# Ternarising feed-forward weights inside the last head group, and tile normalisations on ScalarE

## The chip, the core and the metric

The kernel runs on one core of a Trainium2 chip. The time is device microseconds of one execution. Engines: PE is TensorE, DVE is VectorE, ACT is ScalarE, POOL is GpSimd, SP is the engine that here only issues DMAs.

## The reference

One decoder layer, post-norm, on x of 4 batches x 512 rows x 512 columns, with a layernorm after each residual sum:

1. attention over the feature axis (stage A below);
2. fused self and cross attention with 16 query heads in 8 groups, fp8-rounded inputs and weights, layernorm on each head's q and k (stage B);
3. a feed-forward block whose weights are ternary and whose rows are rounded to integers (stage C):

```python
def _quant_weight(w):
    scale = jnp.clip(jnp.mean(jnp.abs(w)), EPS, None)
    return jnp.clip(jnp.round(w / scale), -1.0, 1.0) * scale
def _quant_act(x):
    scale = 127.0 / jnp.clip(jnp.max(jnp.abs(x), axis=-1, keepdims=True), EPS, None)
    return jnp.clip(jnp.round(x * scale), -128.0, 127.0) / scale
h = bitlinear(x, w_gate_up)            # 512 -> 4096
a, b = jnp.split(h, 2, axis=-1)
h = jax.nn.silu(a) * b
out = _layernorm(x + bitlinear(h, w_down))   # 2048 -> 512
```

(The straight-through terms of the reference are left out here, and `bitlinear` is a product of the rounded rows and rounded weights.) The scale of a weight matrix is a mean over all of it, so no weight can be ternarised before every absolute value has been summed.

## The kernel before

All engines run lists of instructions written out by hand, in order, with semaphores between them; what stands first in an engine's list is done first, even if it has to wait.

**Stage A** takes the first 440 us or so and ends with XQ: the normalised rows, transposed and fp8-rounded in four versions (for q, cross q, k and v). XQ takes 64 KB of each partition.

**Stage B** is a loop over 32 pairs n = 4g + b: head group g (8 of them) and batch b (4). Each pair has four steps st (128 rows each), counted through as T = 4n + st, 0 to 127. In one step PE makes the scores of two heads, the projections of the next pair n + 1 (they read XQ and the weights split in high and low f16 halves: `whq`/`wlq` in two slots, g mod 2), the products of probabilities and values of step T - 1, transposes of probabilities, and the output projection of step T - 2. DVE accumulates the output projection of T - 3 (or T - 2) into x1 (L1086), takes row maxima (L1111), normalises q and k (L1056), scales probabilities (L1066), and rounds the attention rows to fp8 in five operations (L1072 to L1082). ACT makes the exponentials (L805) and copies from PSUM. POOL computes reciprocal deviations. In the last group nothing has to be prepared for a next one; in the last pair there are no projections. x1 is complete for batch b once pair 28 + b has been accumulated.

In each pair ACT also sums absolute values of a 1/32 slice of the feed-forward weights (L785, L786; loads `load_abs` on SP).

**Between B and C.** After the last step DVE adds up these sums, POOL reduces over partitions, and DVE makes the scale (L1162 to L1165). The weights, 12 chunks of 128 x 2048 f32 (1 MB each), are loaded to `wch`, which has 8 slots and lies over stage B's buffers, after the last projection. A chunk is ternarised in three operations: scale and add 1.5 x 2^23 on DVE (`tern_scale`, L1239), subtract it again into bf16 on ACT (L888), clip to -1 and 1 on DVE (`tern_clip`, L1243). 8 chunks are the gate and up weights `wgu`, 4 the down weights `wdn`.

**Stage C** has 16 tiles t of 128 rows. For each: statistics of x1's rows (`x_stats`, L1174, L1177), POOL's deviation (L1356, L1358), normalisation (L1193), row maximum, scales, rounding (`x_prepare`, L1193 to L1201), ACT's subtraction (L865), transposes (L617). Then 32 matmuls of gate and up in four quarters j (L632); ACT's silu of each quarter (L871) and DVE's product (`h_make`, L1207); the maximum over the whole hidden row (L1212), scales, four roundings (L1219), ACT's subtractions (L877), 16 transposes (L642), two copies to hT (ACT), 16 down matmuls (L651), then y (L1225), its statistics, POOL's deviation, normalisation (`y_out`, L1234) and the store. The order is written out in `two_tiles`: PE does the whole of gate and up of tile t + 1, then all transposes of tile t, then its down product. DVE does the reduction and the four roundings of tile t, y of tile t - 1, then the products of tile t + 1 with `x_prepare(t + 2)` behind the second.

## Time and profile before

| | us |
|---|---|
| median of 3 runs (1930.96 to 1931.54) | 1931.26 |
| the profiled execution, its own time | 1932.42 |
| its span, first to last instruction | 1930.6 |

Over the span PE is busy 1790.4 us (93%), DVE 1525.8 (79%), ACT 1052.5 (55%), POOL 262.9 (14%). How to read it: busy time is the sum over instructions, with overlaps taken once; a group's mean duration is longer than the distance from one start to the next when instructions follow each other closely, so the costs of a queue are read from start to start. In a row of a stretch the numbers after its length are busy us and, in brackets, instructions of PE, PE's weight loads, DVE, ACT and POOL, in this order. The clock column behind them is the TensorE clock that was granted, 1.00 being 2.4 GHz and 0.50 being 1.2 GHz.

### The profile page before, as it was taken

How to read it: one execution, taken by the hardware profiler on the slowest of the kernel's cores; microseconds unless marked ns; L12 is line 12 of the kernel's file. 1: busy time of each engine (PE TensorE's matmuls, PEld its weight loads, DVE VectorE, ACT ScalarE, POOL GpSimd, SP SyncE). 2: the span in 40 equal slices, each digit the busy share in tenths (PEclk: the TensorE clock that was granted, in tenths of full speed). 3: DMA queues.
4: the chain of work that ended last, by engine and by line, in shares of the span. 5: the costliest groups of instructions: out<-in, count | busy, mean ns of one | idle time of the engine just before them, and what ended most of it. 6: DMA issues, size and time to landing. Idle time of an engine off the chain costs nothing.

```text
span 1930.6 us, 32318 instructions
## 1 busy us (share of the span) xinstructions
PE 1790.4 (93%) x11024; PEld 1245.1 (64%) x11024; DVE 1525.8 (79%) x4964; ACT 1052.5 (55%) x2526; POOL 262.9 (14%) x361
## 2 busy tenths in 40 slices
PE   7999999448999999999999999999999999759987
PEld 3444444236877777877877877787787887424443
DVE  0175747487888888888898888888889888789997
ACT  1121211225667666776666666766677566566555
POOL 0000000011111112111111111211111111111110
PEclk9999999769999999999999999999999999979999
DMA  6000000201101110100101110111010000420000
GB/s 218 22 1 22 1 0 1 78 1 61 44 22 39 33 33 10 54 28 22 54 20 30 39 36 22 39 33 33 21 51 9 11 11 24 175 81 17 23 23 28
DMA packets 46209, 70.79 MB, mean 37 GB/s; under 512 B 3552, under 2 KB 26592, under 8 KB 45024
## 3 DMA queue, kind: packets, MB, share of 16 engines
q1 hardware_dynamic: 46048, 68.73, 10.7%
q8 instruction: 90, 1.47, 0.3%
q14 instruction: 71, 0.58, 0.1%
HBM read 63.47 MB, written 4.19 MB: 35 GB/s over the span
## 4 chain that ended last, share of the span: by engine, by line
PE 75%; DVE 16%; ACT 5%; issue 2%; DMA 1%; POOL 1%; DVEq 0%; POOLq 0%; ACTq 0%; SPq 0%
PE bank L354 17%; PE bank L410 16%; PE bank L464 10%; PE bank L512 9%; PE bank L549 5%; PE bank L476 5%; PE bank L585 3%; PE bank L470 3%; PE bank L443 3%; DVE am L1212 2%; PE bank L437 1%; ACT hb L877 1%; PE bank L632 1%; DVE hh L1207 1%; ACT hs L871 1%
## 5 line engine op out<-in xcount | busy, mean ns | idle before, releaser
L805 ACT ACTIVATE pr<-bank,nmx 128x512 f32<-128x512 f32 x256 | 175.2, 693 | 148.3 <-DVE nmx L1111 148.2
L512 PE MATMUL bank<-kT,qT 128*128 128x512 f32 x512 | 242.4, 596 | 0.7 <-ACT kT L756 0.7
L464 PE MATMUL bank<-prT,KV 128*128 128x256 f32 x1024 | 242.3, 379 | 0.5 <-ACT prT L680 0.4
L410 PE MATMUL bank<-whq,XQ 128*128 128x256 f16 x1024 | 234.7, 276 | 0.0
L410 PE MATMUL bank<-wlq,XQ 128*128 128x256 f16 x1024 | 234.5, 275 | 0.0
L464 PEld LDWEIGHTS bank<-prT,KV 128*128 128x128 f32 x1024 | 189.5, 190 | 52.5 <-issue 23.0
L1324 POOL TENSOR_TENSOR rdev<-gvar,cst 128x7 f32<-128x7 f32 x128 | 190.2, 1486 | 10.0
L793 ACT ACTIVATE yb<-bank,rsT 128x128 bf16<-128x128 f32 x512 | 146.7, 373 | 66.8 <-PE bank L470 66.8
L1111 DVE TENSOR_REDUCE nmx<-bank 128x1 f32<-128x512 f32 x256 | 167.1, 681 | 8.7 <-PE bank L512 5.2
L1322 POOL TENSOR_TENSOR gvar<-mvB,geps 128x7 f32<-128x7 f32 x128 | 27.3, 214 | 1046.0 <-DVE mvB L1046 1046.0
L680 ACT ACTIVATE prT<-bank 128x512 f32<-128x512 f32 x256 | 153.1, 617 | 13.3 <-PE bank L549 13.3
L549 PE MATMUL bank<-identf,pr 128*128 128x128 f32 x1024 | 150.5, 275 | 9.2 <-DVE pr L1066 8.6
L680 ACT ACTIVATE raw<-bank 128x512 f32<-128x512 f32 x128 | 76.8, 600 | 125.7 <-DVE nq L1056 66.5
L1056 DVE TENSOR_SCALAR nq<-raw,mvB,rdev 128x128 f32<-128x128 f32 x512 | 142.1, 342 | 0.7 <-POOL rdev L1324 0.7
L512 PEld LDWEIGHTS bank<-kT,qT 128*128 128x128 f32 x512 | 92.7, 191 | 72.2 <-issue 61.8
L410 PE MATMUL bank<-whk,XQ 128*128 128x128 f16 x1024 | 126.7, 221 | 9.8 <-DVE wlk L1025 8.6
L476 PE MATMUL bank<-wp,cq 128*128 128x512 bf16 x512 | 132.3, 381 | 2.9 <-DVE x L1086 2.9
L549 PEld LDWEIGHTS bank<-identf,pr 128*128 128x128 f32 x1024 | 118.8, 142 | 23.7 <-DVE pr L1066 21.3
L750 ACT ACTIVATE qT<-bank,hlq 128x256 f32<-128x256 f32 x256 | 133.3, 588 | 1.2 <-PE bank L443 1.1
L1066 DVE TENSOR_SCALAR pr<-pr,ri 128x512 f32<-128x512 f32 x256 | 124.5, 487 | 9.1
L632 PE MATMUL bank<-wgu,xiT 128*128 128x512 bf16 x512 | 119.9, 390 | 9.9 <-ACT hs L871 6.5
L410 PE MATMUL bank<-wlk,XQ 128*128 128x128 f16 x1024 | 126.7, 221 | 0.0
(163 smaller groups left out, 3447.5 us busy)
## 6 DMA issues: line engine op xcount, KB each, us to landing
wst<-in_wcat SPq DMA_DIRECT2D x24, 512.0 KB, 4.0
wpst<-in_wproj SPq DMA_DIRECT2D x8, 1024.0 KB, 5.3
wa<-in_wgu SPq DMA_DIRECT2D x32, 256.0 KB, 2.6
wch<-in_wgu SPq DMA_DIRECT2D x8, 1024.0 KB, 13.2
xT<-in_xT SPq DMA_DIRECT2D x4, 1024.0 KB, 5.3
x<-in_x SPq DMA_DIRECT2D x4, 1024.0 KB, 12.1
wkx<-in_wkvx SPq DMA_DIRECT2D x8, 512.0 KB, 5.0
wa<-in_wdn SPq DMA_DIRECT2D x32, 128.0 KB, 2.6
```

The source lines that it names most:

```text
L354: ins = mm(dst, lhs(k), rhs(k), start=(k == 0), stop=(k == n - 1))
L410: ins = mm(dst, XQ[:, c, k, b * S + j * P:b * S + (j + 1) * P], w, start=(k == 0 and m == 0), stop=(k == KT - 1 and m == 1))
L464: mm(OB[:, 0:2 * P], KV[:, n % 2, t, P:2 * P], prT[:, st % 2, t, :, :].rearrange("p h s -> p (h s)"), start=(t == 0), stop=(t == ST - 1))
L476: ins = mm(P0[:, :], cq[:, T % 2, c * P:(c + 1) * P], wp[:, c, :], start=(c == 0), stop=(c == 3))
L512: mm(SB_[h][:], qT[:, h, st * P:(st + 1) * P], kT[:, :], start=True, stop=True).then_inc(s["scores_made"], 1)
L549: ins = nc.tensor.transpose(TB_[h][:, t * P:(t + 1) * P], pr[:, h, t * P:(t + 1) * P], identf[:])
L680: return act_f(dst, src, ACT.Copy)
L793: ins = act_f(yb[:, T % 2, c * P:(c + 1) * P], OB[:, c * P:(c + 1) * P], ACT.Copy, scale=rsT[:, T // 16, c:c + 1])
L805: act_f(pr[:, h, :], SB_[h][:], ACT.Exp, bias=nmx[:, st, h:h + 1], accum_out=su[:, st, h:h + 1]).then_inc(s["exp_done"], 1)
L1056: ins = v.tensor_scalar(nq[:, j % 2, h * P:(h + 1) * P], raw[:, h * P:(h + 1) * P], mvB[:, h, 0:1], rdev[:, h:h + 1], ALU.subtract, ALU.mult)
L1111: v.tensor_reduce(nmx[:, st, h:h + 1], SB_[h][:], AX.X, ALU.max, negate=True).then_inc(s["max_ready"], 1)
L1324: g.tensor_tensor(rdev[:], gvar[:], CPOW, ALU.pow).then_inc(s["stats_ready"], 1)
```

## The change

1. **Memory.** XQ is laid out by batch. In the last group a batch's part is free once its pair is projected, and `wgu` and `wdn` are written over it. `wch` is gone: chunks are staged in two places that are free in the last group, `wst` (even chunks) and slot 0 of the split weights, now one tensor `wqs` (odd ones).
2. **Sums of absolutes** come in 24 loads of 128 x 1024 in pairs 0 to 23, in place of 32 of 128 x 512 and 128 x 256; POOL's reduction over partitions stands in pair 24, the scale on DVE in pair 25.
3. **Ternarising** is spread by a table TURN over steps of pairs 28 to 31: two chunks in pair 28, three each in 29 and 30, four in 31. In such a step DVE clips the chunk before and scales this one, after rounding the attention rows; ACT subtracts after its probability copies. SP loads chunk c + 2 when ACT has done chunk c.
4. **First tiles.** In the last pair DVE also does `x_stats(0..3)` and, in steps 1 to 3, `x_prepare(0..2)`; ACT the normalisations of tiles 0 to 2 and the subtractions of 0 and 1; PE transposes tile 0 in the last step. PE starts gate and up of tile 0 between the last two output projections.
5. **Normalisations on ACT.** x and y are normalised by an Identity activation with scale 1/deviation and bias -mean/deviation; POOL makes that bias in two more operations.
6. **Order of the loop.** PE puts the first half of tile t's transposes between the third and fourth gate quarter of t + 1, and the second half behind the fourth. DVE puts the four roundings behind the first product, y behind the second and `x_prepare(t + 3)` behind the third. The statistics run four tiles ahead. y has two buffers, xiT three, the scales four.

The diff, cut to its core:

```diff
+NCH = 12
+TURN = {(28, 2): 0, (28, 3): 1, (29, 1): 2, (29, 2): 3, (29, 3): 4, (30, 1): 5, (30, 2): 6, (30, 3): 7,
+        (31, 0): 8, (31, 1): 9, (31, 2): 10, (31, 3): 11}
-        XQ = sb(stageAB, "XQ", [P, 4, KT, NB * S], BF16)
+        XQ = sb(stageAB, "XQ", [P, NB, 4, KT, S], BF16)
-        wch = sb(stC, "wch", [P, NCH, F])
+        def stage(c):
+            if c % 2 == 0:
+                return wst[:, :, :, :].rearrange("p s k n -> p (s k n)")
+            return wqs[:, 0, :, :, :].rearrange("p a k n -> p (a k n)").bitcast(F32)
...
# SP
+            def load_chunk(c):
+                if c < 2:
+                    sp.wait_ge(s["wl_ready"], 6 * NG)
+                    sp.wait_ge(s["proj_q_made"], 4 * (TT - 4))
+                else:
+                    sp.wait_ge(s["tern_int"], c - 1)
...
+                sp.dma_start(dst, src).then_inc(chunk_loaded[c % 2], 16)
...
+                if n == TT - 5:
+                    load_chunk(0)
+                    load_chunk(1)
+                for st in range(ST):
+                    if (n, st) in TURN and TURN[n, st] + 2 < NCH:
+                        load_chunk(TURN[n, st] + 2)
...
# PE, stage C
+            av(LT - 1)
+            pe.wait_ge(s["acc_done"], LT - 2)
+            project_out(LT - 2)
+            turn_x(1, 1)
+            pe.wait_ge(s["tern_made"], 8)
+            gate_up(0, 0, 0, True)
+            gate_up(0, 0, 1, True)
+            pe.wait_ge(s["acc_done"], LT - 1)
+            project_out(LT - 1)
+            gate_up(0, 0, 2, True)
+            gate_up(0, 0, 3, True)
...
+            for t in range(NT):
+                for j in range(4):
+                    if t + 1 < NT:
+                        gate_up(t + 1, (t + 1) % 2, j, False)
+                    if j in (2, 3):
+                        turn_h(t, j - 2)
+                if t + 2 < NT:
+                    turn_x(t + 2, t % 2)
+                down(t)
...
# ACT, pair of stage B
+                    if n == TT - 1 and st == 2:
+                        xi_out(0, 0)
+                    if n == TT - 1 and st == 3:
+                        xt_out(0, 0)
+                        xi_out(1, 1)
+                    if n == TT - 1 and st:
+                        x_norm(st - 1)
+                    if (n, st) in TURN:
+                        tern_out(TURN[n, st])
...
# ACT, stage C
+            for t in range(NT):
+                for j in range(4):
+                    if t + 1 < NT:
+                        silu(t + 1, (t + 1) % 2, j)
+                    if j == 1:
+                        for i in range(4):
+                            hb_out(t, i, t == 0)
+                        if t + 3 < NT:
+                            x_norm(t + 3)
+                    if j in (2, 3):
+                        h_out(t, j - 2)
+                if t + 2 < NT:
+                    xt_out(t + 2, t % 2)
+                if t + 3 < NT:
+                    xi_out(t + 3, (t + 1) % 2)
+                if t:
+                    y_norm(t - 1, (t - 1) % 2)
+            y_norm(NT - 1, 1)
...
+            def x_norm(t):
+                act.wait_ge(s["rstdX_ready"], t + 1)
+                act_f(x1[:, t, :], x1[:, t, :], ACT.Identity, scale=rsC[:, 0:1], bias=nbC[:, 0:1]).then_inc(s["xn_done"], 1)
...
# DVE, pair of stage B
+                    if (n, st) in TURN:
+                        c = TURN[n, st]
+                        if c:
+                            tern_clip(c - 1)
+                        tern_scale(c)
+                    if n == TT - 1 and st:
+                        x_prepare(st - 1, (st - 1) % 2)
+                    if n == TT - 1:
+                        x_stats(st)
...
# DVE, x_prepare: its own normalisation is gone
-                dve.wait_ge(s["rstdX_ready"], t + 1)
-                own.do(v.tensor_scalar(x1[:, t, :], x1[:, t, :], mvC[:, 0, 0:1], rsC[:, 0:1], ALU.subtract, ALU.mult))
+                dve.wait_ge(s["xn_done"], t + 1)
...
# DVE, stage C
+            h_make(0, 0, 0)
+            h_make(0, 0, 1)
+            accumulate(LT - 1, 15)
+            h_make(0, 0, 2)
+            h_make(0, 0, 3)
+            for t in range(NT):
+                h_scales(t, t % 2)
+                for j in range(4):
+                    if t + 1 < NT:
+                        h_make(t + 1, (t + 1) % 2, j)
+                    if j == 0:
+                        for i in range(4):
+                            h_round(t, t % 2, i, t == 0)
+                    if j == 1 and t:
+                        y_make(t - 1, (t - 1) % 2)
+                    if j == 2 and t + 3 < NT:
+                        x_prepare(t + 3, (t + 1) % 2)
+                if t + 4 < NT:
+                    x_stats(t + 4)
+            y_make(NT - 1, 1)
```

## Rows read from the trace of the kernel before

**Rows 1.** The page, chain that ended last, shares by engine.
```profile
PE 75%; DVE 16%; ACT 5%; issue 2%; DMA 1%; POOL 1%; DVEq 0%; POOLq 0%; ACTq 0%; SPq 0%
```

**Rows 2.** Stretches of the run: window, busy per engine (instructions), granted clock, DMA share, GB/s.
```profile
1538.20:1653.80 115.60, 114.09 (x824) 90.57 (x822) 99.36 (x355) 75.74 (x195) 20.46 (x24) 1.00 0.16 61
1644.50:1674.50 30.00, 26.27 (x138) 18.74 (x137) 22.88 (x59) 17.52 (x49) 0.20 (x1) 1.00 0.54 224
1674.50:1719.35 44.85, 15.38 (x63) 6.61 (x62) 35.21 (x65) 29.01 (x25) 8.76 (x7) 0.66 0.27 94
1719.35:1903.12 183.77, 163.99 (x934) 78.43 (x932) 164.17 (x371) 104.95 (x167) 19.29 (x52) 0.98 0.05 18
```

**Rows 3.** Groups of instructions in 1674.5 to 1719.35: count, busy us, mean ns, idle before.
```profile
L1239 DVE TENSOR_SCALAR wch<-wch,winv 128x2048 f32<-128x2048 f32 x12 | 15.2, 1276 | 0.0
L888 ACT ACTIVATE wgu<-wch 128x2048 bf16<-128x2048 f32 x8 | 15.0, 1900 | 11.7 <-DVE wch L1239 11.7
L1243 DVE TENSOR_SCALAR wgu<-wgu 128x2048 bf16<-128x2048 bf16 x8 | 5.5, 690 | 0.0
```

**Rows 4.** Timeline of DVE, pair 29: start, duration, instruction, idle before.
```profile
1597.15 0.75 DVE L1086 SCALAR_TENSOR_TENSOR x<-bank,pscale,x 128x512 f32<-128x512 f32 x1
...
1603.96 0.29 DVE L1072 TENSOR_SCALAR yb<-yb 128x512 bf16<-128x512 bf16 x1 [0.74 <-ACT yb L793]
...
1608.94 0.48 DVE L1066 TENSOR_SCALAR pr<-pr,ri 128x512 f32<-128x512 f32 x1
...
1614.18 0.69 DVE L1132 TENSOR_REDUCE xmx<-bank 128x8 f32<-128x512 f32 x1 [1.19 <-PE bank L585]
```

**Rows 5.** Timeline of PE, the same pair.
```profile
1596.95 1.88 PE L512 MATMUL bank<-kT,qT 128*128 128x512 f32 x4
...
1609.95 0.60 PE L549 MATMUL bank<-identf,pr 128*128 128x128 f32 x4
```

**Rows 6.** Timeline of DVE, one tile of the feed-forward loop.
```profile
1799.05 2.25 DVE L1212 TENSOR_REDUCE am<-hh 128x1 f32<-128x2048 f32 x1
...
1803.43 0.75 DVE L1225 SCALAR_TENSOR_TENSOR y<-bank,am,x 128x512 f32<-128x512 f32 x1
...
1805.22 1.41 DVE L1207 SCALAR_TENSOR_TENSOR hh<-bank,am,hs 128x512 f32<-128x512 f32 x2
1806.55 0.54 DVE L1193 TENSOR_SCALAR x<-x,mvC,rsC 128x512 f32<-128x512 f32 x1
1807.13 0.68 DVE L1196 TENSOR_REDUCE am<-x 128x1 f32<-128x512 f32 x1
...
1808.75 0.74 DVE L1207 SCALAR_TENSOR_TENSOR hh<-bank,am,hs 128x512 f32<-128x512 f32 x1
...
1811.19 0.54 DVE L1234 TENSOR_SCALAR yo<-y,mvC,rsC 128x512 f32<-128x512 f32 x1
...
1812.47 2.25 DVE L1212 TENSOR_REDUCE am<-hh 128x1 f32<-128x2048 f32 x1
```

**Rows 7.** Timeline of PE behind the last pair.
```profile
1679.87 1.89 PE L476 MATMUL bank<-wp,cq 128*128 128x512 bf16 x4 [2.94 <-DVE x L1086]
...
1706.95 5.42 PE L632 MATMUL bank<-wgu,xiT 128*128 128x512 bf16 x16 [2.92 <-DVE wgu L1243]
```

**Rows 8.** Waits in 1759 to 1890: who for whom, us in total, times, longest.
```profile
PE bank L651 <- ACT hT L680: 13.0, 11, 1.2
```

**Rows 9.** Line 1212, the reduction over a hidden tile: duration ns, first and last start.
```profile
L1212 DVE TENSOR_REDUCE am<-hh x16: 2253/2253/2286, 1719.3 to 1914.6; 128x1 f32<-128x2048 f32 x16
```

**Rows 10.** Timeline of POOL, one tile.
```profile
1812.63 0.19 POOL L1356 TENSOR_TENSOR vC<-mvC,cst 128x1 f32<-128x1 f32 x1 [6.61 <-DVE mvC L1177]
```

**Rows 11.** Groups of the whole run, line 756.
```profile
L756 ACT ACTIVATE kT<-bank,hln 128x512 f32<-128x512 f32 x32 | 25.5, 796 | 1.2 <-PE bank L449 1.2
```

**Rows 12.** Groups of the whole run, table loads.
```profile
L680 ACT ACT_TABLE_LOAD x1 | 1.3, 1283 | 15.6 <-PE bank L354 15.6
L871 ACT ACT_TABLE_LOAD x1 | 1.3, 1283 | 0.0
```

More of the change, by code:

```diff
@@ L471, in av, with turn_x @@
                 ins.then_inc(s["av_made"], 1)
+            def turn_x(t, par):
+                pe.wait_ge(s["xi_made"], t + 1)
+                if par or not (isinstance(t, int) and t == 0):
+                    pe.wait_ge(s["xit_out"], t)
+                for k in range(KT):
+                    ins = nc.tensor.transpose(MBh[:, k * P:(k + 1) * P], xib[:, k * P:(k + 1) * P], identb[:])
+                ins.then_inc(s["xit_made"], 1)
             def project_out(T):
@@ L647, in down, with turn_h @@
+            def turn_h(t, u):
+                pe.wait_ge(s["hb_ready"], 4 * t + 2 * u + 2)
+                if t:
+                    pe.wait_ge(s["ht_out"], 2 * t + (u - 1))
+                half = bank[4 + u][:, :].bitcast(BF16)
+                for c in range(8):
+                    ins = nc.tensor.transpose(half[:, c * P:(c + 1) * P], hb[:, (8 * u + c) * P:(8 * u + c + 1) * P], identb[:])
+                ins.then_inc(s["ht_made"], 1)
+            def down(t):
+                if t:
                     pe.wait_ge(s["y_ready"], t)
@@ L877, in hb_out @@
                 act_f(hb[:, j * D:(j + 1) * D], hi_[:, j * D:(j + 1) * D], ACT.Copy, bias=-INT_ROUND).then_inc(s["hb_ready"], 1)
-            def h_out(t, first):
-                for u in range(2):
-                    act.wait_ge(s["ht_made"], 2 * t + u + 1)
-                    if u == 0 and not first:
-                        act.wait_ge(s["dn_made"], t)
-                    copy(hT[:, 8 * u:8 * u + 8, :], bank[4 + u][:, :].bitcast(BF16).rearrange("p (c s) -> p c s", c=8)).then_inc(s["ht_out"], 1)
@@ L893, in _, with y_norm @@
+            def y_norm(t, par):
+                act.wait_ge(s["rstdY_ready"], t + 1)
+                if t >= 2:
+                    act.wait_ge(out_stored[par], 16 * (t // 2))
+                act_f(yo[:, par], y[:, par], ACT.Identity, scale=rsC[:, 1:2], bias=nbC[:, 1:2]).then_inc(s["yo_ready"], 1)
+            xt_out(1, 1)
+            xi_out(2, 0)
             for j in range(4):
                 silu(0, 0, j, True)
-            def two_tiles(t0, first, last):
-                for par in range(2):
-                    t = t0 + par
-                    f = first and par == 0
-                    more = not (last and par == 1)
-                    for j in range(4):
-                        hb_out(t, j, f)
-                    for j in range(4):
-                        if more:
-                            silu(t + 1, 1 - par, j)
-                        if j == 2 and not last:
-                            xi_out(t + 2, par)
-                    h_out(t, f)
-                    if not last:
-                        xt_out(t + 2, par)
@@ new lines, in x_stats, with x_prepare @@
+            def x_stats(t):
+                stats(x1[:, t, :], 0, s["varX_ready"])
+            def x_prepare(t, par):
+                dve.wait_ge(s["xn_done"], t + 1)
+                own.do(v.tensor_reduce(am[:, 0, 0:1], x1[:, t, :], AX.X, ALU.max, apply_absolute_value=True))
+                own.sync()
+                scales(t, 0)
+                if par or not (isinstance(t, int) and t == 0):
+                    dve.wait_ge(s["xi_made"], t)
+                v.tensor_scalar(xi[:], x1[:, t, :], am2[:, t % 4, 2:3], INT_ROUND, ALU.mult, ALU.add).then_inc(s["xi_added"], 1)
@@ L1213, in h_scales @@
                 own.sync()
-                scales(par, 1)
+                scales(t, 1)
             def h_round(t, par, j, first):
```

360 lines of the change are left out of this document (136 added, 224 removed).

## The prediction

> **What bounds the kernel now.** I read the page's chain first: three quarters of it is TensorE, 16% VectorE [rows 1]. An average over stages is no use for a change at the end, so next came the table of stretches [rows 2]. Three regimes are to be seen. In head pairs 28 to 30 (1538.2 to 1653.8) PE is busy 114.1 of 115.6 us and DVE 99.4: PE-bound, DVE with little room. In the last pair, without projections, PE has 26.3 of 30.0 and DVE 22.9. From 1674.5 to the first reduction over a hidden tile at 1719.35 PE has 15.4 of 44.9 at a granted clock of 0.66: this stretch belongs to ternarising and the first tiles. In the tile loop PE and DVE are level, 164.0 and 164.2 of 183.8 us, 11.7 each per tile, yet a tile takes 13.1.
>
> **What the ternarising costs.** A chunk is one scaling (1.28 us), one ScalarE copy (1.90) and one clip (0.69) [rows 3]; on DVE scaling and clip take 1.8 start to start. Twelve are 21.6 us of DVE and 22.8 of ACT. The change removes none of it, but moves it under pairs 28 to 31, with the preparation of tiles 0 to 2 and the statistics of tiles 0 to 3.
>
> **Pairs 28 to 30: plus 9.9 us.** In DVE's order the chunk stands ahead of the next accumulation and the next row maxima, and PE waits for both. The margins: accumulation L1086 ends at 1597.9, and PE reaches the projection that needs it after its scores L512 (1596.95 and 1.88, less an overlap), at about 1598.7: 0.8 us. The scaled rows L1066 end at 1609.4, PE's transposes L549 start at 1609.95: 0.5. DVE's idle gaps behind those places are 0.74 before L1072 and 1.19 before L1132 [rows 4, 5]. Pair 29, three chunks: after the first, DVE is 1.8 late and PE hardly; after the second 3.6, the accumulation arrives 2.8 beyond its margin and PE is 2.8 late; the 0.74 gap closes; after the third DVE is 4.65 late and PE 4.15. So 5.4 us of work gives 4.1 of delay. Pair 30 likewise 4.1; pair 28, with one scaling (its clip comes later) and one whole chunk (3.0 us), 1.7. ACT's copy starts when the scaling ends and takes 1.9, while DVE comes to the next maximum after 1.4; the exponentials are so 0.5 later than DVE's own delay, and DVE needs them only after its normalisations, so I price that at nothing. Bounds: 4 us, if the margins hold at every step, and 26, where each chunk costs DVE and ACT in series (8 x 3.7 less three times 1.2). I take 9.9, nearest to the margins read.
>
> **Last pair: plus 14.0 us.** Step 0 gets a chunk and one tile's statistics (1.8 + 0.82), of which the 1.19 gap takes up one part: 1.4. Steps 1 to 3 get chunk, preparation (1.62 without its normalisation) and statistics: 4.3 each [rows 6]; of the waits there only about 0.5 is given back, so 12.6. Bounds: 10 (twice as much given back) to 20 (PE, idle for some 4 us per step, falls to 1.2 GHz and its part of the chain doubles). ACT's normalisation (0.8) fits before the preparation, since DVE first does 1.8 of chunk.
>
> **Tail: 13.6 us in place of 44.85.** From the end of pair 31 on DVE, now 1674.5 + 23.9 = 1698.4: accumulation 0.7; PE has by then been idle for over 10 us and starts at 1.2 GHz, as in the trace, where the last output projection took 1.89 and the first 16 gate matmuls 5.42, both behind a long gap [rows 7]. So: projection 1.9, transposes 0.6, eight matmuls 3.4, eight more 1.9 with the clock returning, projection 0.9, sixteen 3.4, last product 0.8. ACT's table load falls beside the first matmuls. First hidden reduction at 1712.0 instead of 1719.35. **Net of these three: minus 7.3.**
>
> **Tile loop and end: minus 21.1 us.** One tile of DVE, from each start to the next [rows 6]: reduction, scales and four roundings 4.38; y and its statistics 1.79; two products 1.33; x normalisation 0.58; rest of the preparation 1.62; y normalisation and x statistics 1.28, of which 0.46 is the first (0.54 less the overlap) and 0.82 the second. With two further products and a wait for ACT's silu this is 13.1 to 13.4. The change takes out 0.58 and 0.46, and the wait, since rounding stands between the products: DVE needs 4.38 + 1.79 + 4 x 0.68 + 1.62 + 0.82 = 11.3. PE needs its 11.7 [rows 2]; what it waited was 13.0 us in ten tiles for hT before the down projection [rows 8], and this goes as well: the first eight transposes now stand before the last gate quarter, whose 1.7 us covers the copy of the first half, and eight down matmuls cover the second. ACT is busy 105.0 us in the 14 tiles [rows 2], 7.5 each, and 8.9 with two normalisations of 0.7 net. Between DVE's 11.3 and PE's 11.7 I take PE's, plus 0.7 once for the first tile: 14 x 11.7 + 0.7 = 164.5 where it was 183.8. The last interval has no preparation: 9.1 for 11.5, since the reductions run from 1719.3 to 1914.6 [rows 9]. The end behind it was 16.0; two more short POOL operations (0.19 each, [rows 10], with their signals about 0.5) and the slower engine make it 16.6. So 190.2 for 211.3.
>
> Is it right to give ScalarE the normalisation? The row speaks against it operation by operation: DVE takes 0.54 [rows 6], ACT's Identity with two per-row operands 0.80 [rows 11]. By price alone the change would lose 0.26 x 32 = 8 us; as DVE is 13.1 long and ACT 8.9, I count it as a gain of 1.0 per tile. The Trainium skill ("ScalarE: Activation LUTs", Rules for kernel authors) says to use VectorE, not ScalarE, for multiply and add. By that rule the loop would not get shorter by this edit; the trace agrees with its price, and not with its use here.
>
> Elsewhere: sums of absolutes go from 32 loads to 24 of the same total size, free before and after (ACT is busy 75.7 of 115.6 us in the pairs), the new layout of XQ changes no instruction's size, and SP's queue reaches each chunk load two steps before it is needed. At nothing; if a load came late, DVE would stand in front of everything in the last pair.
>
> **Sum.** -7.3 - 21.1 = -28.4. The profiled execution took 1932.4 (span 1930.6), 1.2 above the median of 1931.3. From the median: 1903.
>
> **Rivals.**
> *Pairs stall in series.* Each chunk delays PE by DVE's 1.8 and ACT's 1.9. For it: DVE is busy 86% there and its idle gaps are waits of a chain; against: DVE doesn't need the exponentials at once. 16 us more: 1919. Chance 0.17.
> *The tile stays bound by a chain.* Reduction, rounding, ACT's copies, then x normalisation ahead of the third silu, in one ACT queue: if the third silu comes 0.9 late in each tile, 12.6 per tile: +12.6, 1915. For: ACT starts rounding only when DVE gives it; against: by my times the silu and DVE arrive together. Chance 0.15.
> *Slower: tables.* ACT loaded a table twice in the whole run, at the start and before the first silu, 1.28 each [rows 12]. Identity ran with Exp's table; no row shows it with Silu's. If they do not share one, each tile has Silu to Identity and back twice: 4 x 1.28 = 5.1 on ACT, 14.0 per tile, over 13.1 from the second load on and so slower than before: 14 x 14.0 = 196, and with the loads in the tail and end about 1938. The change would then not move the normalisation off the path but lengthen it. The Trainium skill (same page, Table sets: the hidden batching unit) says cheap functions such as identity are in every set; by it this rival falls. Chance 0.03.
> *Both first rivals at once*: 1931, no change. 0.03.
> *Better*: DVE's work in the pairs hides (4 instead of 9.9) or the loop goes below PE's count: 1893 to 1898. 0.10.
> The forecast itself keeps 0.52.
>
> **How the numbers follow.** Range: low 1893 (pairs at 4 and last pair at 10). High 1918: nearly reaches the first rival and holds the second. About 0.2 is outside. A measurement of this kernel can tell some 0.2%, 4 us: faster 0.94 (the forecast, the first two rivals and the better case), same 0.03 (both rivals), slower 0.03 (tables).
>
> **What would show it.** Right: the ternarising copies lie between about 1540 and 1690, three per pair, and pairs 29 and 30 are 42 to 43 us long; the first hidden reduction starts at 1712 +- 5; the reductions are 11.7 apart; DVE no longer waits for silu and PE's wait for hT is gone; still two table loads. Wrong: pairs of over 46 us, a DVE wait for ACT's x normalisation or for a chunk load in the last pair, intervals over 12.3 in the loop, or more than two table loads.

## The result, and the profile after

The changed kernel takes 1904.17 us (median of 4 runs, 1903.54 to 1905.79) where the kernel before, beside it, takes 1931.4 (1930.96 to 1931.68): a ratio of 0.986, 95% interval 0.984 to 0.988. Forecast were 1903, and a range of 1893 to 1918. The profiled execution took 1905.79, with a span of 1902.8 (before: 1932.42 and 1930.6), so the difference to be found in the two traces is 27.8 us of span.

To cut both traces at the same places I use two instructions that occur once in each unit of work: the exponential of the cross scores (px, once per pair, in its first step) and the reduction over a hidden tile (once per tile).

| from start to start | before | after | difference | forecast |
|---|---|---|---|---|
| start to px of pair 24 | 1382.44 | 1381.40 | -1.0 | 0 |
| px 24 to px 25 | 39.12 | 45.47 | +6.35 | 0 |
| px 25 to px 28 | 116.69 | 116.68 | 0.0 | 0 |
| px 28 to px 31 | 115.52 | 128.53 | +13.0 | +11.3 |
| px 31 to first hidden reduction | 65.58 | 44.50 | -21.1 | -18.65 |
| first to last hidden reduction | 195.28 | 169.60 | -25.7 | -21.7 |
| last hidden reduction to the end | 16.0 | 16.6 | +0.6 | +0.6 |
| sum | | | -27.8 | -28.4 |

The forecast of each row regroups its terms (step 0 of the last pair, 1.4, belongs to the row of px 28 to px 31). The start to px 24 is where single executions differ: 1380.1 to 1382.9 over the kernels of this study. The sum is right within 1 us, its parts are not: +6.35 in pair 24 was priced at nothing, and the last pair with the tail and the tile loop gave 2.45 and 4.0 more than forecast. The 4.0 hides two errors of its own: the 14 tiles up to the last reduction but one took 158.1 us where 164.5 were forecast, and the last interval took 11.48 where 9.1 were forecast.

The table of stretches of the kernel after (columns as in [rows 2]); the stretches are px 24 to px 25, px 28 to px 31, px 31 to the first reduction, and 14 tiles:

```profile
1381.40:1426.87 45.47, 41.40 (x282) 32.94 (x280) 34.65 (x123) 27.56 (x70) 7.33 (x9) 0.92 0.10 30
1543.55:1672.08 128.53, 117.65 (x824) 90.96 (x821) 114.37 (x374) 87.48 (x191) 26.14 (x28) 0.99 0.20 67
1672.08:1716.58 44.50, 33.53 (x149) 21.99 (x150) 34.90 (x82) 27.46 (x52) 3.21 (x12) 0.88 0.13 48
1716.58:1874.70 158.12, 157.24 (x936) 79.41 (x934) 147.05 (x321) 120.51 (x191) 26.66 (x100) 1.00 0.06 21
```

The last line answers to the last of [rows 2]: 14 tiles take 158.1 in place of 183.8 us, and PE is busy in all but 0.9 of them. DVE has gone from 164.2 to 147.1, ACT from 105.0 to 120.5. The second line shows the price: in the pairs PE now stands 10.9 us of 128.5, where it stood 1.5 of 115.6. The third: the 33.5 us of PE work between px 31 and the first hidden reduction (33.1 before) now lie in 44.5 us and no longer in 65.6.

**The tile loop.** The waits of 58 us of it (1795 to 1853), which answer to [rows 8]:

```profile
POOL vC L1364 <- DVE mvC L1136: 45.2, 10, 6.1
ACT hs L901 <- PE bank L640: 13.2, 10, 1.6
DVE hh L1257 <- ACT hs L901: 1.7, 5, 0.3
```

PE waits for nobody there; its wait for hT (13.0 us before) is gone. DVE's timeline over one tile, against [rows 6]:

```profile
1796.55 2.25 DVE L1262 TENSOR_REDUCE am<-hh 128x1 f32<-128x2048 f32 x1
...
1800.01 1.67 DVE L1269 TENSOR_SCALAR hi_<-hh,am 128x512 f32<-128x512 f32 x4
...
1804.27 0.75 DVE L1257 SCALAR_TENSOR_TENSOR hh<-bank,am,hs 128x512 f32<-128x512 f32 x1 [0.33 <-ACT hs L901]
...
1808.03 2.25 DVE L1262 TENSOR_REDUCE am<-hh 128x1 f32<-128x2048 f32 x1
```

11.48 from reduction to reduction, with one gap of 0.33 us in front of a product. DVE would need 11.15, PE's work fills 11.48: the bound is PE. The same work looked like more in the kernel before. Four of its inner tiles:

```profile
1825.54:1877.80 52.26, 47.35 (x274) 22.70 (x272) 47.63 (x109) 30.19 (x49) 5.93 (x16) 1.00 0.06 21
```

PE is busy 11.84 per tile there, at a granted clock of 1.00 as in after; the 0.98 of [rows 2] comes from the first tile alone, 0.76 from 1719.35 to 1733.40. A gate or down matmul follows the one before it by 216 ns in both kernels. Nearly all of the 0.36 between 11.84 and 11.48 is in the records of two matmuls: in these tiles of before PE stops twice (1.18 us for hT, 0.05 between two gate quarters), and the record of the matmul in front of each stop is 0.16 longer than where the next one follows at once.

**The tail.** It begins with DVE's first accumulation behind the last pair, forecast 33.3 us after px 31 and found 33.9 after it:

```profile
1705.95 0.72 DVE L1114 SCALAR_TENSOR_TENSOR x<-bank,pscale,x 128x512 f32<-128x512 f32 x1
```

Where [rows 7] show the first 16 gate matmuls in 5.42 us, PE's timeline of after has

```profile
1706.72 1.04 PE L498 MATMUL bank<-wp,cq 128*128 128x512 bf16 x4 [1.94 <-DVE x L1114]
1707.60 0.39 PE L492 MATMUL bank<-identb,xib 128*128 128x128 bf16 x4
1707.82 3.62 PE L640 MATMUL bank<-wgu,xiT 128*128 128x512 bf16 x16
```

The projection takes 1.04 (1.89 before) and the gate 3.62: both as long as at the upper level of the clock. PE had waited 1.9 us before them, where in the kernel before it had worked 5.6 us of the 32.5 from 1674.5 to 1707.

**Pair 24.** POOL's timeline around the reduction over partitions, and the waits beside it:

```profile
1391.77 1.53 POOL L1335 TENSOR_TENSOR rdev<-gvar,cst 128x7 f32<-128x7 f32 x1
1399.17 0.41 POOL L1346 PARTITION_ALL_REDUCE asum<-asum  x1 [5.87 <-issue]
1406.94 0.20 POOL L1333 TENSOR_TENSOR gvar<-mvB,geps 128x7 f32<-128x7 f32 x1 [7.37 <-issue]
```

```profile
POOL gvar L1333 <- issue: 7.4, 1, 7.4
...
DVE kn L1082 <- POOL rdev L1335: 5.4, 1, 5.4
...
PE bank L463 <- DVE nq L1084: 3.7, 1, 3.7
```

An operation of 0.41 us occupies POOL for 13.6 us, since it stands still for 5.9 in front of it and 7.4 behind, though the next deviation's input is there 5.8 us before it starts. That deviation of q and k comes late, DVE waits 5.4 us for it, PE 3.7 for DVE, and the granted clock of the pair is 0.92 where before it was 1.00 throughout. PE stands 4.07 us in this pair (0.43 before) and is busy 41.40 (38.69 before): of the 6.35, some 3.6 are waiting and 2.7 the lower clock. The five kernels of this study that have the reduction in step 1 took 43.7 to 45.7 for this pair, so 6.35 is near the upper end of what it costs (4.6 to 6.6).

**Pairs 28 to 30.** Pair 28 (two chunks) is 1.66 longer, pair 29 (three) 4.08, as forecast (1.7 and 4.1). The third interval, pair 30 and step 0 of pair 31, is 7.27 longer, forecast 5.5. PE's timeline in pair 30 shows what was added:

```profile
1642.20 1.91 PE L424 MATMUL bank<-wqs,XQ 128*128 128x256 f16 x16
...
1650.61 2.83 PE L424 MATMUL bank<-wqs,XQ 128*128 128x256 f16 x16 [2.16 <-DVE x L1114]
1653.24 2.69 PE L478 MATMUL bank<-prT,KV 128*128 128x256 f32 x8
```

Behind a wait of 2.16 us for DVE's accumulation the same sixteen projections take 2.83 in place of 1.91, and eight products of probabilities and values 2.69 in place of 1.89 (both at full clock one step before): 1.7 us by the lower clock. A wait of this size does not always have that effect. In pair 29 PE waits 2.05 us at the same place, both in after and in the kernel of experiment 3 below, whose instructions up to there are the same. The pair in after, and in that kernel:

```profile
1584.06:1626.68 42.62, 39.20 (x292) 31.01 (x291) 38.38 (x126) 28.50 (x62) 8.55 (x8) 1.00 0.23 75
```

```profile
1581.49:1625.77 44.28, 40.70 (x289) 32.04 (x290) 38.47 (x126) 28.51 (x62) 8.55 (x8) 0.96 0.21 73
```

The second one's clock fell and its pair is 1.66 longer. A difference of up to 1.7 us between single stretches of two traces can be this alone.

ACT loaded a table twice, as in [rows 12], and Identity in the loop costs what the row of before said (0.80):

```profile
L816 ACT ACTIVATE x<-x,nbC,rsC 128x512 f32<-128x512 f32 x16 | 12.9, 804 | 0.0
L692 ACT ACT_TABLE_LOAD x1 | 1.3, 1283 | 14.7 <-PE bank L368 14.7
L901 ACT ACT_TABLE_LOAD x1 | 1.3, 1283 | 0.0
```

### The profile page after: what moved, and what is told of

The parts are those of the page before. It is cut to its first block, busy times and chain, and to the rows that moved or that the text cites. A ratio compares the mean times of both kernels' runs of the same rounds, so it can differ in the third digit from the quotient of the medians.

```text
span 1902.8 us, 32280 instructions
## 1 busy us (share of the span) xinstructions
PE 1789.1 (94%) x11024; PEld 1251.0 (66%) x11024; DVE 1506.1 (79%) x4917; ACT 1065.9 (56%) x2478; POOL 269.1 (14%) x417
## 3 DMA queue, kind: packets, MB, share of 16 engines
q1 hardware_dynamic: 40288, 68.73, 10.9%
## 4 chain that ended last, share of the span: by engine, by line
PE 71%; DVE 15%; issue 8%; POOL 2%; ACT 2%; DMA 1%; POOLq 0%; SPq 0%; DVEq 0%; ACTq 0%
PE bank L368 18%; PE bank L424 14%; PE bank L478 10%; PE bank L534 8%; PE bank L573 5%; PE bank L498 4%; PE bank L609 3%; PE bank L484 3%; PE bank L457 2%; PE bank L451 1%; DVE nq L1084 1%; DVE nmx L1190 1%; ACT yb L823 1%; PE bank L542 1%; POOL rsC L1369 1%
## 5 line engine op out<-in xcount | busy, mean ns | idle before, releaser
L424 PE MATMUL bank<-wqs,XQ 128*128 128x256 f16 x2048 | 249.5, 276 | 4.4 <-DVE x L1114 4.4
L424 PEld LDWEIGHTS bank<-wqs,XQ 128*128 128x128 bf16 x2048 | 199.6, 100 | 45.4 <-issue 15.7
L640 PE MATMUL bank<-wgu,xiT 128*128 128x512 bf16 x512 | 115.7, 379 | 0.1
```

The lines of the kernel that those rows point to most:

```text
L424: ins = mm(dst, XQ[:, b, c, k, j * P:(j + 1) * P], w, start=(k == 0 and m == 0), stop=(k == KT - 1 and m == 1))
```

## The experiments

Each kernel is the one after the change with the edit shown. The span of the profiled execution stands in brackets behind the time.

**1. POOL's reduction where POOL has room.** Behind the fourth deviation of a pair POOL is idle for some 15 us (its longest wait for DVE in 1543 to 1672 is 16.4).

```diff
-                    if n == NABS and st == 1:
+                    if n == NABS and st == 3:
                         pool.wait_ge(s["abs_ready"], 1)
```

> The changed kernel with one edit: POOL's reduction over partitions stands behind the deviation of step 3 of pair 24, not of step 1. Theory: in the changed kernel this reduction kept POOL for 13.6 us (5.9 of issue before it, 7.4 behind it), the next deviation came 5.7 late and pair 24 took 45.5 us in place of 39.1. Behind step 3 POOL has 16.6 us until its next work, so the pair goes back to 39.1 and the kernel gets 6.3 us faster, about 1898. Rival: pair 24 is long for another reason (DVE's two sums, the load of the absolutes' last slice); then it stays at 45 and the time at 1904. Second rival: the 13.6 us run over into step 0 of pair 25 and the wait moves there: pair 24 at 39, pair 25 longer by up to 6.

1898.38 us (1897.74 to 1899.97; span 1896.9), ratio to before 0.983, interval 0.982 to 0.984. px 24 to px 25 is 39.13 again, every later interval is within 0.02 us what it was in after. POOL's timeline:

```profile
1407.90 1.48 POOL L1335 TENSOR_TENSOR rdev<-gvar,cst 128x7 f32<-128x7 f32 x1
1415.38 0.41 POOL L1346 PARTITION_ALL_REDUCE asum<-asum  x1 [6.01 <-issue]
1425.06 0.21 POOL L1333 TENSOR_TENSOR gvar<-mvB,geps 128x7 f32<-128x7 f32 x1 [9.27 <-DVE mvB L1074]
```

The 6.0 in front are there again, but the next deviation now waits for its data (it starts 0.09 us after them), and no longer for POOL. So the lengthening of pair 24 is the place of this one instruction. Its second rival falls too, since px 25 to px 28 is 116.69 as before. With it in step 3 the change brings 33.5 us (beside 1931.89) in place of 27.2.

**2. What belongs to the reduction and what to the change of kind**, on top of experiment 1.

```diff
+                        own.do(g.partition_all_reduce(asum3[:], asum2[:], P, RADD))
+                        own.sync()
                         g.partition_all_reduce(asum3[:], asum2[:], P, RADD).then_inc(s["absum_ready"], 1)
```

> e1_reduce_gap (1898.4 us) with POOL's reduction over partitions issued twice in a row, the second from the same source to the same place. My theory: the 5.9 us before the reduction and the 7.4 behind it belong to the change of POOL from ordinary operations to this one and back, not to the operation, so the second one starts within a microsecond of the end of the first, and the whole stays at 1898 to 1899. Rival: each reduction carries its own 5.9 in front; then the second starts 6 us after the first, POOL comes back to its deviations about 1429.6 where e1_reduce_gap began the next at 1425.1, DVE and PE wait, and the whole is 4 to 5 us longer, 1903.

1899.31 us in one run (span 1897.2). POOL's timeline:

```profile
1415.96 0.43 POOL L1346 PARTITION_ALL_REDUCE asum<-asum  x1 [5.98 <-issue]
1416.50 0.40 POOL L1348 PARTITION_ALL_REDUCE asum<-asum  x1
1425.67 0.21 POOL L1333 TENSOR_TENSOR gvar<-mvB,geps 128x7 f32<-128x7 f32 x1 [8.77 <-DVE mvB L1074]
```

The second starts 0.54 us after the start of the first, and it had to wait until the first was complete. The 6 us belong to the first use after other operations, not to each reduction; and the stillness behind is not the reduction itself running on longer than its record of 0.41 says. What the stillness behind is made of no run shows: here the next deviation waits for its data, 8.8 us. The Trainium skill ("GPSIMD Engine Reference", Instruction dispatch) says that the first call to a freshly loaded kernel pays about 6 us for the loading of its code, with no instruction to be seen in the profile; the trace agrees, with 5.9 to 6.0 in three kernels. But it was not this program's first reduction: one stands in stage A, at 16.9 us in after, and the price was paid anew. In the kernel before, POOL's timeline has the reduction between the stages:

```profile
1668.39 0.20 POOL L1335 TENSOR_TENSOR asum<-asum 128x8 f32<-128x8 f32 x1 [25.18 <-ACT wa L786]
1674.71 0.41 POOL L1351 PARTITION_ALL_REDUCE asum<-asum  x1 [6.12 <-DVE asum L1157]
1683.66 1.13 POOL L1356 TENSOR_TENSOR vC<-mvC,cst 128x1 f32<-128x1 f32 x1 [8.54 <-DVE mvC L1177]
```

It had been idle for 6.1 us when the sums came, and the reduction started 0.14 us after them; and it was idle for 8.5 behind it until the next statistics, and started 0.09 after those: whatever both sides cost lay under waits.

**3. Normalisations of the loop back on DVE**, all else as in after.

```diff
# ACT, stage C
-                        if t + 3 < NT:
-                            x_norm(t + 3)
-                if t:
-                    y_norm(t - 1, (t - 1) % 2)
-            y_norm(NT - 1, 1)
# DVE, x_prepare from t = 3 on; y likewise ahead of x_stats(t + 4)
+                    v.tensor_scalar(x1[:, t, :], x1[:, t, :], mvC[:, 0, 0:1], rsC[:, 0:1], ALU.subtract, ALU.mult).then_inc(s["xn_done"], 1)
```

> The changed kernel with the normalisations of the tile loop (x of tiles 3 to 15, y of all) back on VectorE, each 0.54 us; everything else, the new order too, as changed. Theory: PE's 11.5 per tile is the bound after the change and DVE is at 11.3; with 1.04 more DVE is at 12.35 and becomes the bound, so tiles come every 12.4 us and the kernel is 10 to 13 us slower than the changed one, about 1916. Rival: the order of the loop alone brought the gain and DVE's queue still has room: 11.5 to 11.7 per tile and 1904 to 1907.

1910.53 us (1910.33 to 1911.85; span 1908.7), ratio 0.989, interval 0.988 to 0.991. The tiles are 12.08 apart. Ten of them, in the table of stretches:

```profile
1738.68:1859.32 120.64, 115.77 (x668) 57.24 (x681) 116.93 (x259) 76.57 (x120) 22.27 (x80) 1.00 0.06 23
```

DVE is busy 116.9 and PE 115.8 of 120.6, and PE waits for the rounded rows again. First to last reduction is 176.0 in place of 169.6: 6.4 us for the whole loop, which is also the difference of the medians. (In the two traces pair 24 is 1.75 shorter and pair 29, by its clock, 1.66 longer; the two nearly cancel, and the end is 0.7 longer.) So of the 1.6 us per tile that the change takes out, the new order alone gives 1.0 (13.07 to 12.08) and the normalisations 0.6 (to 11.48). I had put the latter at 1.0, and this experiment at 10 to 13 us.

**4. PE's transposes of the hidden tile all behind the fourth gate quarter**, and ACT's copies behind the fourth silu.

```diff
-                    if j in (2, 3):
-                        turn_h(t, j - 2)
+                turn_h(t, 0)
+                turn_h(t, 1)
```

> The changed kernel with PE's old place for the transposes of the hidden tile (all 16 behind the fourth gate quarter) and ACT's two copies to hT behind its fourth silu. Theory: PE again waits about 1.2 us per tile for hT before the down product, so 12.5 to 12.7 per tile and 15 us slower, about 1919. Rival: what made PE wait was DVE's length, and with the normalisations gone from DVE the place of the transposes does not matter: 11.5 to 11.8 per tile, 1904 to 1908.

1913.93 us in one run (span 1911.8), tiles 12.17 apart. The waits in the loop of this kernel:

```profile
PE bank L658 <- ACT hT L692: 3.8, 5, 0.8
DVE hh L1257 <- PE bank L640: 3.6, 5, 0.7
```

PE's wait for hT before the down product is back, 0.76 per tile, and with it the 0.69 by which a tile is longer. That splitting the transposes is what removes it, is so shown by itself. The tile is 0.4 shorter than I expected, since the wait is 0.76 per tile here and 13.0 / 11 = 1.2 in [rows 8].

**5. Is it DVE or ACT that makes the pairs longer?** The scalings and clips in pairs 28 to 30 are cut to 8 of 2048 columns, with ACT's copies at full size; so most of the gate and up weights stay unternarised.

```diff
-                            tern_clip(c - 1)
-                        tern_scale(c)
+                            tern_clip(c - 1, n < TT - 1)
+                        tern_scale(c, n < TT - 1)
```

> The changed kernel with DVE's scalings and clips of the chunks in pairs 28 to 30 cut to 8 of 2048 columns (so most gate and up weights are not ternarised); ACT's copies and the loads stay whole. Theory: the delay there (from the exponential of pair 28 to that of pair 31 it takes 128.5 us, 115.5 before the change) comes from DVE's 1.8 us per chunk standing ahead of the accumulation and the maxima; ACT's 1.9 are hidden. Then the stretch is 117 us or less (step 0 of pair 31 still carries its chunk), 11 us gained, about 1893. Rival (each chunk costs DVE and ACT in series): ACT's 8 x 1.9 stay on the path and the stretch is 122 to 125.

1893.13 us in one run (span 1891.3). The stretch px 28 to px 31:

```profile
1543.48:1660.54 117.06, 113.82 (x815) 90.51 (x821) 103.03 (x374) 87.18 (x192) 21.61 (x28) 1.00 0.22 74
```

117.1 in place of 128.5. Pairs 28 and 29 take 38.86 and 38.52, what they took before (38.86 and 38.52), with ACT's copies of 1.9 us in them. ACT's part was free, DVE's was all of it: 11.5 us for 8 chunks (with what the waits bring by the clock). The third interval is 39.67 where it was 38.13; the 1.5 over are the full chunk and the statistics in step 0 of pair 31, forecast 1.4.

**6. Accumulation ahead of the chunk.** If DVE's delay reaches PE by certain places only, moving the nearest one should help.

```diff
                     if (n, st) in TURN:
                         c = TURN[n, st]
+                        if st:
+                            accumulate(T - 2, (T - 2) % 16)
```

(and the same accumulation is left out at the start of the next step)

> Edit: in the steps with a chunk (but for the first step of a pair) DVE accumulates the output projection of T - 2 ahead of the clip and the scaling, in place of at the start of the next step. Nothing else is changed, POOL's reduction stays in step 1 of pair 24. My theory: the two places at which a chunk makes PE late are the accumulation (PE's next output projection waits for it) and the row maxima; with the first one ahead of the chunk, only the second is left, which had 0.5 us of room where the accumulation had 0.8. PE's wait of 2.2 us for the accumulation in pair 30 goes, and with it the granted clock of 0.66 right behind it. Pairs 28 to 30 and step 0 of pair 31 come to about 124 us in place of 128.5, the whole to 1900 to 1901. Rival A: DVE's 1.8 us per chunk reach PE by the maxima in any case, and the place of the accumulation changes nothing: 128 and 1904. Rival B: the output projection of T - 2 is not ready when DVE gets there, so that DVE waits in front of the chunk: over 130 and 1906 or more, with a DVE wait for PE's bank at the accumulation in the rows.

1907.1 us in one run (span 1905.2): nothing gained. px 28 to px 31 is 129.05. The end behind the last hidden reduction is 1.7 longer than in after, though nothing was edited there: the last 16 down matmuls take 5.30 in place of 3.61, behind the same waits, at the lower clock. The waits in 1540 to 1672 of this kernel,

```profile
PEld bank L573 <- DVE pr L1094: 9.5, 9, 2.4
PE bank L573 <- DVE pr L1094: 6.2, 5, 1.9
PEld bank L424 <- DVE x L1114: 2.7, 2, 1.6
```

and those of 1543 to 1672 in after:

```profile
PEld bank L424 <- DVE x L1114: 6.9, 3, 3.0
PEld bank L573 <- DVE pr L1094: 5.7, 5, 1.5
PE bank L424 <- DVE x L1114: 4.4, 3, 2.2
PE bank L573 <- DVE pr L1094: 3.7, 5, 1.0
```

PE's wait for the accumulation has shrunk and its wait for the scaled probabilities has grown by nearly as much. PE's wait in pair 30 is 0.73 in place of 2.16, and the lower clock behind it is gone, as six us of both traces show (first after, then this kernel; the clock stands third from the end):

```profile
1650.00:1656.00 6.00, 5.39 (x27) 4.36 (x28) 5.31 (x21) 3.77 (x6) 1.65 (x3) 0.72 0.48 161
```

```profile
1650.00:1656.00 6.00, 4.87 (x34) 4.07 (x34) 5.77 (x15) 3.47 (x6) 2.31 (x2) 1.00 0.07 9
1650.76 1.92 PE L424 MATMUL bank<-wqs,XQ 128*128 128x256 f16 x16 [0.73 <-DVE x L1114]
```

This third interval is 0.8 shorter; pairs 28 and 29 are 0.4 and 0.9 longer, with the clock at 1.00 in both kernels. Rival A holds: the place is not what matters. That DVE's sum is what does fits this and experiment 5. With experiment 1 together:

> The edit of e6_acc_first together with the one of e1_reduce_gap (POOL's reduction in step 3 of pair 24). The two act in stretches that are 150 us apart and share no wait, so their gains should add: 1898.4 less what e6_acc_first gains. By my theory 1894 to 1895, by rival A 1898, by rival B over 1900.

1898.92 us (1897.84 to 1902.26; span 1896.9), ratio 0.984, interval 0.982 to 0.985: the same as experiment 1, as rival A has it. The three intervals are as with experiment 6 alone (40.95, 43.52, 44.63), and so is the long end.

**7. Three chunks out of the last pair**, on top of experiment 1.

```diff
-TURN = {(28, 2): 0, (28, 3): 1, (29, 1): 2, (29, 2): 3, (29, 3): 4, (30, 1): 5, (30, 2): 6, (30, 3): 7,
-        (31, 0): 8, (31, 1): 9, (31, 2): 10, (31, 3): 11}
+TURN = {(28, 1): 0, (28, 2): 1, (28, 3): 2, (29, 0): 3, (29, 1): 4, (29, 2): 5, (29, 3): 6, (30, 0): 7,
+        (30, 1): 8, (30, 2): 9, (30, 3): 10, (31, 0): 11}
```

> e1_reduce_gap (1898.4 us) with another table of chunks: (28,1) to (28,3) have 0 to 2, (29,0) to (29,3) 3 to 6, (30,0) to (30,3) 7 to 10, and (31,0) has 11. Three chunks leave steps 1 to 3 of the last pair and go to pairs 28, 29 and 30. My theory: a chunk in the last pair costs all of DVE's 1.8 us, since DVE is the bound there, and one in the pairs with projections 4.08 / 3 = 1.36, the measured lengthening of pair 29 by its three: 3 x (1.36 - 1.8) = -1.3, and 1897. Rival A: the first step of a pair has 1.2 us of idle DVE before the maxima of the cross scores, so chunks there cost only about 0.6: -3.6 in all, 1895. Rival B: in the first step the clip and scaling stand ahead of the cross softmax and ACT's copy ahead of its exponential, so that a chunk there costs both engines' 1.8 and 1.9 in series: +5, 1903. Last pair to first hidden reduction: 44.5 less 5.4 by all three, so about 39 to 40.

1902.67 us (1901.67 to 1904.22; span 1899.8), ratio 0.985, interval 0.984 to 0.986: 4.3 slower than experiment 1, near rival B. The last pair with the tail gave back 3.4 (41.15 for 44.52), not 5.4: 1.1 per chunk. px 28 to px 31 went from 128.55 to 135.17, so three more chunks cost 6.6 there, 2.2 each, more than DVE's own 1.8. They do not cost the same: a chunk in step 0 stands ahead of px, so the first interval has two more (43.48 for 40.53, 1.5 each), the second one more (46.28 for 42.62, 3.7) and the third as many as before (45.41 for 45.40). One thing speaks for rival B's series, ACT's timeline in step 0 of pair 29:

```profile
1578.25 1.91 ACT L802 ACTIVATE wgu<-wqs 128x2048 bf16<-128x2048 f32 x1 [1.84 <-DVE wqs L1162]
...
1580.79 0.63 ACT L881 ACTIVATE px<-px 128x512 f32<-128x512 f32 x1
```

ACT waits 1.84 for DVE's scaling, then copies, and only then comes to the exponential of the cross scores. Another thing can explain the amount as well: the second interval's granted clock is 0.97 where it was 1.00, and in pair 29 of experiment 3 such a fall was worth 1.66 with no chunk added. Without that much, the three cost some 1.65 each. The two were not separated by a run. In the first interval, where two more chunks cost 3.0 together, rival B's 3.7 for the one in step 0 is not borne out, though its time came near. Nor did a chunk in the last pair cost 1.8, as my theory had it.

**8. The scaling on ACT**, on top of experiment 1. If DVE's sum is the price, the scaling should leave DVE.

```diff
# ACT, tern_out
+                act_f(stage(c), stage(c), ACT.Identity, scale=winv[:, w:w + 1], bias=cst[:, 6, 0:1]).then_inc(s["tern_scaled"], 1)
# DVE
-                        tern_scale(c)
```

> e1_reduce_gap (1898.4 us) with the scaling of all twelve chunks taken from DVE and put on ACT, as an Identity activation with scale 1/mean and bias 1.5 x 2^23, directly ahead of ACT's subtraction; DVE keeps the clip. My theory, from e4_no_dve_part and e6_acc_first: what makes the pairs long is the sum of DVE's work, wherever it stands, and ACT has room. In after's rows of 1543 to 1672 ACT waits 13.1 us in all in front of the 8 subtractions for DVE's scaling (1.6 each), so that with 1.9 of its own in place of the wait it ends 0.3 later per chunk. DVE loses 1.2 of 1.8 per chunk, and the 0.6 left is about its margin: pairs 28 to 30 with step 0 of pair 31 come to 118 to 120 us in place of 128.5, the last pair and the tail to about 42 in place of 44.5, and the whole to 1886 to 1889. Rival: ACT is the next bound of a step, since in 9 of 12 steps it does not wait for the maxima before its exponentials; each chunk then costs its 1.9 us more of ACT, three of them 5.7 in a pair against the 4.1 of DVE: 129 to 133, and 1898 to 1903.

1894.16 us (1893.33 to 1895.66; span 1891.5), ratio 0.981, interval 0.980 to 0.982. The best of the kernels that compute everything, by 4.2 us against experiment 1. The two intervals overlap by 0.001, but the slowest of its four runs (1895.66) is faster than the fastest of experiment 1 (1897.74). The traces say where the gain is: 2.5 in the pairs (126.04 for 128.55), 1.4 in the last pair and the tail (43.15 for 44.52). Most of the 2.5 goes with the clock. Pair 28 is even longer (41.39 for 40.53), pair 29 is 0.5 shorter, and the third interval takes 42.58 in place of 45.40 at a granted clock of 1.00 in place of 0.96: PE's wait for the accumulation in pair 30 is 1.34 there, and the fall of the clock (1.7 by the rows above) does not come. I had forecast 1886 to 1889. From the groups of ACT (6 of the 12 scalings), and the waits of 1537 to 1660:

```profile
L804 ACT ACTIVATE wqs<-wqs,cst,winv 128x2048 f32<-128x2048 f32 x6 | 12.9, 2142 | 0.0
```

```profile
DVE ri L1096 <- ACT pr L839: 8.4, 8, 1.8
PEld bank L573 <- DVE pr L1098: 7.0, 4, 2.3
```

The scaling takes ACT 2.14 us, not 1.9, and a wait that after did not have among its long ones is now there: DVE waits eight times, 8.4 us in all, for ACT's exponential. ACT was free while its part was one copy (experiment 5) and is a second bound with two operations per chunk.

> The same for chunks 0 to 7 alone; chunks 8 to 11, in the last pair, are scaled by DVE as in the kernel after. It tells the two places apart. My theory: the pairs as in e10_act_scale (118 to 120 us), the last pair and the tail as in e1_reduce_gap (44.5): 1888 to 1891, 2 us over e10_act_scale. Rival: in the last pair ACT also has the normalisations of tiles 0 to 2 and the rounding of tiles 0 and 1, which DVE's preparation waits for; 1.9 us more ahead of the next step's exponentials there cost more than DVE's 1.2 gave, and this kernel is 1 to 3 us faster than e10_act_scale.

1897.33 us (1896.38 to 1899.27; span 1897.2), ratio 0.982, interval 0.981 to 0.984. Pairs 28 and 29 as in the kernel with all twelve (41.41 and 42.10), then 43.40 up to px 31 and 45.40 from there to the first hidden reduction, against 42.58 and 43.15. So in the last pair, too, it is better to have the scaling on ACT, by about 3 us (3.2 by the medians, and no runs of the two overlap); the rival of this run falls. Against experiment 1 the first eight alone bring about 1 us, and there the runs do overlap: most of the gain comes from the last four.

## Why the prediction was right

Its sum of -28.4 against -27.8 measured is partly luck: +6.35 not priced and +1.7 too little in the pairs stand against 4.0 and 2.45 too little gain behind them, and 1.0 of the start. The forecast of the time, 1903 for 1904.17, is so close because these cancel. By its steps:

- **Pairs 28 to 30, plus 9.9.** The mechanism and the method hold. With margins of 0.8 and 0.5 and gaps of 0.74 and 1.19 read from [rows 4, 5], two chunks cost 1.66 and three 4.08 (forecast 1.7 and 4.1). What is nothing in it, ACT's copy, is nothing (experiment 5), which settles the rival of a stall in series for this table of chunks. Pair 30 was forecast 4.1 and came to 5.7: the third interval of 45.40 against 39.67 in experiment 5. The 1.6 agrees with the lower clock behind PE's wait of 2.16 (1.7 by its rows). The step had taken PE's waiting as time lost once, and not as something that also slows what comes behind it.
- **Last pair and tail, 14.0 and 13.6.** DVE's first accumulation behind the last pair starts 33.9 after px 31; forecast were 20.7 + 12.6 = 33.3. So "4.3 each, 0.5 given back" was right as a sum. Its terms are not confirmed: a chunk taken out of the last pair gave back 1.1 and not 1.8 (experiment 7), and PE, which waits 3.6, 4.5 and 2.2 us there, runs at a granted clock of 0.84 from 1675 to 1706.7, which only the upper bound of 20 had thought of. The tail took 10.6, not 13.6: the step "PE has by then been idle for over 10 us and starts at 1.2 GHz" failed. That was read from [rows 7], the kernel before, where the ternarising stood between; with the preparation moved into the pair PE had waited only 1.9 us, and 16 gate matmuls took 3.62. (Why the full clock is there by 1706 was not tested by itself; the trace shows it.) Long gaps in the trace of before were carried over to a kernel in which they had been filled.
- **Tile loop, 14 x 11.7 + 0.7 and 9.1.** Which engine bounds it, which waits go, and that the tables stay put: all as forecast. The size was off by 4.0 (169.6 against 173.6), in two parts that partly cancel. The 14 tiles took 158.1, not 164.5: PE's 11.7 was its busy time, and this contains ends of records that are there only because PE waits; from start to start its work is 11.48 (3.1 us in 14 tiles). The rest is the 0.7 for the first tile and tiles at both ends that are shorter (11.33 and 11.29, 10.77 and 10.00). The last interval took 11.48, not 9.1: the 9.1 is DVE's shorter work without a preparation, but PE is busy throughout this interval and bounds it too. The gain of 1.0 per tile from moving the normalisations was 0.6; the order of the queues gave the other 1.0 (experiments 3 and 4). DVE's 11.3 by the rows of before is 11.15 in after. The Trainium skill's rule ("ScalarE: Activation LUTs", Rules for kernel authors) of multiply and add on VectorE holds for the price of the operation (0.80 against 0.54) and fails here for the kernel: with it the tile is 12.08 and not 11.48.
- **"Elsewhere ... at nothing".** This is the step that failed. It priced the sums of absolutes and the loads, and left out that POOL's reduction moved from a place where POOL waited anyway to the middle of a pair, where POOL makes a deviation in each step that DVE and then PE wait for. The duration of the instruction, 0.41, says nothing about it, and the idle time around it in the trace of before (6.1 and 8.5) did not show it either, since both ended with the data that POOL waited for. The instructions of a moved step were counted for DVE, ACT, PE and SP, and not for POOL. With the reduction elsewhere the kernel is at 1898.4 (experiment 1).
- **Rivals.** Pairs that stall in series: no (experiment 5). The tile bound by a chain at 12.6: no, 11.48. Tables: no, two loads. These had their signs in the places named. The better case came in part: the loop went below PE's count of 11.7.

No single one of these errors would have carried the time out of the range: without the 6.35 the kernel is at 1898.4, and with the loop as long as forecast it would be near 1908.

## What to carry to other kernels

When a step is moved, count its instructions on every engine, the cheapest too, and ask what would come late if one of them took far longer than its duration: here 0.41 us of POOL held 13.6 us, free at a join of two stages and worth 5 to 6 us inside a pipeline. Work put under a bound engine is paid for by the sum on the engine that feeds it, less its margins; moving it about within that engine's queue only moved the wait (experiments 6 and 7), moving it to the next engine helped until this one had its own waits (experiment 8). Take what an engine needs per unit of work from start to start and not from its busy time, which holds a little more at every wait. And before a difference of 1 or 2 us between two traces is explained, compare the granted clock of the stretch in both.

## What was not expected of the hardware

- The reduction over partitions has 5.9 to 6.2 us of stillness in front of it, though its input is there, and 7.0 to 7.6 behind it before POOL takes the next ordinary operation, in the five kernels where that one's input is there earlier. Both run while POOL waits: where the data come later, POOL starts 0.1 after them. A second reduction right behind the first starts 0.54 after it (experiment 2).
- A wait of 2.2 us of PE in the middle of dense work was followed by a stretch at the lower clock level (0.72 on the mean from 1650 to 1656); in experiment 6 a wait of 0.7 at the same place was not (1.00). In the tail a wait of 1.9 us was followed by matmuls at full speed. The length of a wait does not decide it: with the same instructions and waits, pair 29 ran at 1.00 in after and at 0.96 in experiment 3 (1.66 us longer), and the last down product took 3.61 in after and 5.30 in experiment 6.
- Identity with two per-row operands takes ACT 0.80 us for 128x512 and 2.14 for 128x2048, where Copy with a constant, written as bf16, takes 1.91.
